# Second layer laid out anew on every engine, with turned contexts kept in DRAM

## What is computed

```python
x = x + L0_xattn(layernorm(x), ctx, key mask)          # 16 heads of 8, biases
x = x + L0_ffn(layernorm(x))                           # 8 experts, the best 2 per row
x = x + L1_xattn(layernorm(x), ctx, query mask)        # below
x = x + L1_ffn(layernorm(x))                           # relu(x @ w1 + b1) @ w2 + b2

def L1_xattn(x, context, mask):
    k, v = split(context @ Wkv); q = x @ Wq
    dots = q k^T * 64**-0.5 - (1 - mask) * 1e6         # mask on the query row
    return softmax(dots) @ v @ Wout + bout
```

## Time and profile before

| | us |
|---|---|
| median of 3 runs (lowest, highest) | 933.73 (932.86, 934.0) |
| the profiled execution | 935.8 |
| its span, from first to last instruction | 934.1 |

### The profile page before, as it was taken

The page is one execution under the profiler, slowest core; times in us unless marked ns, Lnnn a source line. Parts: engine busy times, 40 slices in busy tenths (PEclk is TensorE's granted clock), DMA queues, the critical chain, the costliest instruction groups (busy, mean ns, idle before and its releaser), DMA issues.

```text
span 934.1 us, 28124 instructions
## 1 busy us (share of the span) xinstructions
PE 838.8 (90%) x7885; PEld 748.4 (80%) x7885; DVE 672.0 (72%) x2052; ACT 673.9 (72%) x2662; POOL 453.1 (49%) x765
## 2 busy tenths in 40 slices
PE   5899999999989789999985788889899999999985
PEld 3677888787777689999984788778788888889874
DVE  5789999999988432222236877878898888988862
ACT  2999999999989423333357877787788887888860
POOL 3135545545444521111156566666666667667441
PEclk9999999999999989999997898899999999999987
DMA  5897777778777122222215666676677777777761
GB/s 165 240 247 230 227 238 238 226 237 247 229 247 179 35 88 68 67 68 73 85 34 166 212 209 199 204 222 215 198 231 225 226 219 204 238 223 234 212 208 45
DMA packets 160451, 171.93 MB, mean 184 GB/s; under 512 B 16052, under 2 KB 139318, under 8 KB 160374
## 3 DMA queue, kind: packets, MB, share of 16 engines
q1 hardware_dynamic: 153474, 156.77, 55.0%
q0 software_dynamic: 6112, 13.90, 5.7%
q10 hardware_dynamic: 788, 0.39, 0.1%
HBM read 90.87 MB, written 80.13 MB: 183 GB/s over the span
## 4 chain that ended last, share of the span: by engine, by line
PE 56%; DVE 10%; issue 9%; ACT 9%; DMA 7%; SPq 4%; POOL 3%; DVEq 0%; ACTq 0%; POOLq 0%
PE bank L1376 7%; PE bank L1383 7%; PE bank L1426 6%; PE bank L1217 6%; ACT PR L701 6%; PE bank L1171 5%; PE bank L1416 4%; PE bank L1209 4%; PE bank L1404 3%; DMA turned_blocks<-BT 3%; ACT PR L708 3%; DVE nmx L894 3%; PE bank L1328 3%; PE bank L1288 2%; PE bank L1193 2%
## 5 line engine op out<-in xcount | busy, mean ns | idle before, releaser
L701 ACT ACTIVATE PR<-PR,nmx 128x128 f32<-128x128 f32 x512 | 197.4, 401 | 0.0
L347 POOL TENSOR_TENSOR PR<-PR,rden 128x512 f32<-128x512 f32 x128 | 133.1, 1040 | 118.4 <-DVE rden L899 118.4
L701 ACT ACTIVATE PR<-bank,nmx 128x128 f32<-128x128 f32 x512 | 187.8, 431 | 0.4 <-DVE nmx L894 0.4
L701 ACT ACTIVATION_READ_ACCUMULATOR PR<-bank,nmx 128x1 f32 x512 | 139.0, 271 | 0.0
L1404 PE MATMUL bank<-XCT,wqk 128*128 128x128 f32 x832 | 115.5, 289 | 14.1 <-DVE YT L1055 10.0
L1404 PEld LDWEIGHTS bank<-XCT,wqk 128*128 128x128 f32 x832 | 103.3, 198 | 22.3 <-DVE YT L1055 11.4
L894 DVE TENSOR_REDUCE nmx<-PR 128x4 f32<-128x512 f32 x128 | 81.5, 679 | 49.8 <-ACT PR L708 49.7
L795 ACT ACTIVATE H<-bank 128x512 f32<-128x512 f32 x70 | 41.8, 597 | 90.3 <-PE bank L1376 90.3
L701 ACT ACTIVATION_READ_ACCUMULATOR PR<-PR,nmx 128x1 f32 x512 | 103.2, 202 | 0.0
L1171 PEld LDWEIGHTS bank<-ident,PR 128*128 128x128 f32 x512 | 60.9, 142 | 39.6 <-issue 37.6
L708 ACT ACTIVATE PR<-bank,fill_q 128x512 f32<-128x512 f32 x128 | 77.8, 688 | 20.4 <-PE bank L1416 20.2
(11 more groups left out here) (182 smaller groups left out, 2050.7 us busy)
## 6 DMA issues: line engine op xcount, KB each, us to landing
turned_blocks<-BT SPq DMA_DIRECT2D x64, 512.0 KB, 4.0
w<-turned_blocks SPq DMA_DIRECT2D x256, 128.0 KB, 3.1
second_layer_values<-wide SPq DMA_DIRECT2D x32, 512.0 KB
wide<-second_layer_values SPq DMA_DIRECT2D x32, 512.0 KB, 5.6
expert_outputs<-HF SPq DMA_DIRECT2D x32, 256.0 KB
expert_outputs<-HF SPq DMA_DIRECT2D x64, 128.0 KB, 2.2
KBD<-expert_outputs SPq DMA_DIRECT2D x64, 128.0 KB
QS<-expert_outputs SPq DMA_DIRECT2D x32, 256.0 KB
```

Of the source, the lines that this page charges most:

```text
L347: nc.gpsimd.tensor_tensor(unit, unit, rden[:, p, G * g:G * g + G].unsqueeze(2).broadcast_to([P, G, P]), ALU.mult).then_inc(s["nm"], 1)
L701: last = nc.scalar.activation(PR[:, g, j * P:(j + 1) * P], scored, ACT.Exp, bias=nmx[:, p, h:h + 1], accum_out=den[:, p, h:h + 1])
```

## The change

Three things are changed; what is computed stays.

- **Turned contexts.** In the first layer the SyncE queue stores each turned context `XCT[:, p, 1, :]` to a new DRAM tensor, one transfer of 64 KB for each sequence. The second layer loads from there into `XCT` directly: its `transpose_in` turns XN alone. The early contexts are loaded turned as well, and `turn_contexts` and `read_contexts` go.
- **Order in a step.** Every engine's `step1` is rewritten. Units 2 and 3 of a sequence are reduced and exponentiated in the next step; the turns of all four units stand in the next step; the XND of a sequence comes one step later, early in it; the projection of quarter 2 of sequence n + 1 stands before the scores of n.
- **Banks and readers.** Quarters 0 to 3 go to banks 5, 4, 4, 6 (before 4, 5, 6, 4), and heads to banks 6 and 5. ScalarE reads quarter 2 and VectorE reads 0, 3 and 1. The experts' rows are added one step earlier, and both halves of the turned blocks are loaded one behind the other after the second half's store.

```diff
 SyncE, step0 (first layer) and step1
+                if exists(n + 2):
+                    wait_apart(sp, (a["xct"], n + 3))
+                    sp.dma_start(ct_dram[n + 2], XCT[:, p, 1, :]).then_inc(a["cst"], 16)
...
                 if exists(n - 1):
+                    wait(sp, c["pv"], NU * (n - 2))
+                    sp.dma_start(V1[:, q, :, :].rearrange("p h d -> p (h d)"), v_dram[n - 1]).then_inc(c[f"v{q}"], 16)
+                if exists(n + 2) and not early(n + 2):
+                    wait(sp, c["y"], NU * n + NU)
+                    sp.dma_start(XCT[:, p, 1, :], ct_dram[n + 2]).then_inc(c[f"ctx{p}"], 16)
+                if exists(n - 1):
+                    store_blocks(n - 1, 1)
                     load_turned(n - 1, 0)
-                    store_blocks(n - 1, 1)
-                if exists(n + 2) and not early(n + 2):
-                    load_ctx(sp, c, n + 2, p)
-                if exists(n):
-                    wait(sp, c["pv"], NU * (n - 1))
-                    sp.dma_start(V1[:, p, :, :].rearrange("p h d -> p (h d)"), v_dram[n]).then_inc(c[f"v{p}"], 16)
-                if exists(n - 1):
                     load_turned(n - 1, 1)
 ScalarE, step1
-                if exists(n):
-                    act.wait_ge(c["y"], NU * n + NU)
...
                 if exists(n + 1):
-                    read_xct(c, n + 1, q, not early(n + 1), c["y"], NU * n)
+                    read_xct(c, n + 1, q, False, c["y"], NU * n)
+                if exists(n - 1):
+                    fill_rows(n - 1, 3)
+                    exponentials(c, n - 1, q, 2)
+                    exponentials(c, n - 1, q, 3)
+                if exists(n + 1):
+                    act.wait_ge(c["y"], NU * (n + 1) + 2)
...
+                if exists(n):
+                    fill_rows(n, 0)
+                    fill_rows(n, 1)
                 if exists(n - 2):
                     read_heads(n - 2, p, 0)
                     read_heads(n - 2, p, 1)
                 if exists(n):
-                    for g in range(NU):
-                        fill_rows(n, g)
-                    for g in range(NU):
-                        exponentials(c, n, p, g)
+                    exponentials(c, n, p, 0)
+                    fill_rows(n, 2)
+                    exponentials(c, n, p, 1)
 GpSimd, step1
-                if exists(n - 1):
-                    scale_pool(pool, c, n - 1, q, 3)
...
+                if exists(n - 2):
+                    scale_pool(pool, c, n - 2, p, 3)
+                if exists(n + 1):
...
+                    nc.gpsimd.tensor_tensor(xrow, xrow, out_bias[:, 0, :], ALU.add).then_inc(c["bias"], 1)
...
+                if exists(n - 1):
+                    scale_pool(pool, c, n - 1, q, 0)
+                if exists(n - 3):
+                    norm_pool(pool, d, n - 3, q)
...
+                if exists(n - 1):
+                    scale_pool(pool, c, n - 1, q, 1)
+                    scale_pool(pool, c, n - 1, q, 2)
 TensorE, step1
+                    wait(pe, c["x"], upto(n - 3))
+                    transpose_in(c, n + 1, q, False)
...
+                    project_y(n, p, 3)
+                    if not early(n):
+                        wait(pe, d["x"], upto(n - 4))
+                        wait(pe, c["yq"], upto(n))
+                        project_y(n, p, 1)
+                if exists(n + 1):
+                    pe.wait_ge(c["xct"], n + 2)
...
+                        project_y(n + 1, q, 0)
...
+                    project_y(n + 1, q, 2)
```

More of the change, by code:

```diff
@@ L1172, in transpose_unit @@
                 last.then_inc(s["t"], 1)
-            def turn_contexts(group, contexts, first_bank, other_bank):
-                pe.wait_ge(ld_kv if group == 0 else ld_gate, 32)
-                count = KEYS_A if group == 0 else KEYS_AHEAD - KEYS_A
-                for i in range(count):
-                    turned = nc.tensor.transpose((first_bank[:, i * P:(i + 1) * P] if i < 4 else other_bank[:, (i - 4) * P:(i - 3) * P]),
-                                                 contexts[:, i, :], ident[:])
-                turned.then_inc(set_pe, 1)
-            def project_keys(m, half):
-                first, out = (0, (bank[6], bank[1])) if m < KEYS_A else (KEYS_A, (bank[0], bank[1]))
-                if m == first:
-                    pe.wait_ge(set_copy, 3 if m < KEYS_A else 4)
-                else:
-                    pe.wait_ge(kg["kc"], 2 * m + half - 1)
+            def project_keys(m, half):
+                first, out, contexts = (0, (bank[6], bank[1]), CTX_A) if m < KEYS_A else (KEYS_A, (bank[0], bank[1]), CTX_B)
+                if m == first and half == 0:
+                    pe.wait_ge(ld_kv if m < KEYS_A else ld_gate, 32)
+                wait(pe, kg["kc"], 2 * m + half - 1)
                 for j in range(G):
@@ L1193, in project_keys @@
                     projected = mm(out[half][:, j * P:(j + 1) * P], wqk1[:, 1, chunk * P:(chunk + 1) * P],
-                                   CT[:, m - first, :], start=True, stop=True)
+                                   contexts[:, m - first, :], start=True, stop=True)
                 projected.then_inc(kg["k"], 1)
@@ L1385, in _ @@
             total = starts[NE]
-            turn_contexts(1, CTX_B, bank[3], bank[6])
             for m in range(KEYS_A, KEYS_AHEAD):
@@ L1405, in project_y @@
                                   XCT[:, p, 1 - g // 2, :], start=True, stop=True)
-                    last.then_inc(c["y"], 3 if g == 2 and early(m) else 1)
+                    last.then_inc(c["y"], 2 if early(m) else 1)
                 def scores(m, p, pair):
@@ L1425, in values @@
                             half = slice(DH1 * r, DH1 * r + DH1)
-                            last = mm(bank[5 + pair][half, j * P:(j + 1) * P].rearrange("p (i b) -> p i b", i=4),
+                            last = mm(O1_BANK[pair][half, j * P:(j + 1) * P].rearrange("p (i b) -> p i b", i=4),
                                       V1[:, p, 2 * (G * pair + j) + r, :], PTC[:, pair, :, G * r + j, :], start=True, stop=True)
@@ L1451, in step1 @@
                     pe.wait_ge(c[f"v{p}"], loads(n - 2, p))
-                    if not early(n):
-                        wait(pe, c["yc"], upto(n, 3, 0))
+                    wait(pe, c["yc"], upto(n, 3, 2))
                     if isinstance(n, int):
@@ L1457, in step1 @@
                     wait(pe, c["pt1"], 64 * (n - 1))
-                    wait(pe, c["yc"], upto(n, 3, 2))
+                    if not early(n + 1):
+                        wait(pe, c["yc"], upto(n + 1, 3, 0))
                     if isinstance(n, int):
```

219 lines of the change are left out of this document (95 added, 124 removed).

## The result

The changed kernel takes 889.91 us (884.11 to 891.61, 4 runs) where the kernel before takes 933.87 us beside it: a ratio of 0.9515, 95% interval 0.9467 to 0.9562. The forecast was 893.7 us. The sum was close, but several of its terms were not. The profiled execution took 891.61 us, its span is 890.0 us.

What follows compares the result with a forecast made beforehand. Steady steps were taken as nearly TensorE's own, early ones as a ring of waits. Terms -20.6, -7.7, -14.0 and +2.2 sum to -40.1: 934.1 to 894.0, less 0.4 for the median, 893.7 us; range 878 to 913.

Steps and rivals of the forecast that it cites:

- Early steps: Second layer, sequences 3 to 11: the wait for XND goes, steps fall from 13.58 to 11.0 us; -20.6 us.
- One sign that I had named: ScalarE in the second layer: its copies should show no waits of a microsecond.
- Turned blocks: Second-layer loads behind the second store: 8.9 us fit before the values need them, 1 to 3 us spare; cost 0.
- rival D: Turned blocks come late for the values in every step, 1.9 us of wait each; 953 us, slower; chance 0.06.
- Steady steps: Second layer, sequences 11 to 31: context transpose and bank wait go, steps fall from 13.00 to 12.3 us; -14.0 us.
- Ramp: First three steps of the second layer: three rounds of ScalarE's 10.5 us, 31.5 instead of 39.25; -7.7 us.
- SyncE's queue: First layer: the added store's issue holds up loads behind it, 0.56 us in four steps; +2.2 us.
- Between the stages: Before the second layer's first scores: 2.0 us of context transposes and copies go, hidden by sequence 1's late rows; 0 us.
- Tail: End of the second layer: later last exponentials against an earlier store of the last half; 0 us, ends -4 and +3.
- Rival B: Second layer: GpSimd holds up one more VectorE instruction by 0.7 us a step; 907 us; chance 0.15.
- Rival C: Early steps: TensorE's clock still falls once in each, so they take 11.9 us; 901 us; chance 0.09.
- Rival F: Second layer: waits only move to the next engine, both kinds of step keep their length; 934 us; chance 0.03.

Runs made afterwards that it cites:

- XND put back: Changed kernel with XND's normalisation moved from third in VectorE's step to right ahead of the copy into XDT; 966.39 us, ratio 0.9937 to the kernel before.
- the small load: Changed kernel with the second layer's load of values cut from 512 KB to 32 KB a step; 878.66 us against the changed kernel's 884.46.
- the kernel with fewer matmuls: Changed kernel without 3 of 4 matmuls of one projection group in the 20 steady steps; 890.06 us against the changed kernel's 884.46.
- the store two places ahead: Changed kernel with the first layer's store of turned contexts issued two places earlier in SyncE's step; 906.59 us, ratio 0.9357 to the kernel before.
- the second run: The changed kernel measured again, unaltered; 884.46 us where the kernel before takes 932.43, ratio 0.9481.

## Why the prediction was right, point by point

- **Early steps, -20.6 forecast, -17.0 measured (13.58 to 11.46).** The mechanism was right and is shown: XND put back takes 1.4 us a step, and the wait of the earlier trace rows is 0.2 us at most. The 11.0 us were missed by the term that I had set to nothing, the turned blocks: 7.1 / 8 = 0.9 us a step. Without them an early step would have 10.6 us; with the small load it has 10.65, of which 0.35 are still such waits. One sign that I had named failed with it: ScalarE's copies of heads waited up to 1.4 us for values whose blocks were late.
- **Turned blocks, 0 forecast.** The step of the prediction that failed: "4.0 + 1.8 + 3.1 = 8.9 us fit, with 1 to 3 us to spare". I added landings of the old, slower steps. With the same bytes in 11 us the store takes 4.5 and the loads 4.1 to land (4.0 and 3.1 in the earlier trace rows), and eight issues take 4.9 to 6.5 us together; the spare time is gone. It was rival D in small: not 1.9 us in each step but 0.9 in the early ones and almost none in the steady ones.
- **Steady steps, -14.0 forecast, -25.4 measured (13.00 to 11.73), past the term's end of -18.** "That puts TensorE at 12.88 - 0.74 = 12.14 us" was too high: its work is 11.60. I had taken the 12.88 us less the listed wait for work. A listed wait is shorter than what it costs: in the kernel with fewer matmuls 0.67 us of them (6 of the rows' matmuls, 0.112 us from start to start) went, the step lost 0.04 us, and the listed wait was 0.52. And the row of 24 matmuls from 770.70 to 773.78 us, which I read as three groups of 1.03 us of work, holds a wait. Its matmuls start 0.112 us apart, which makes 0.89 a group; once there are 0.41 us between two of them, where TensorE stood for the final addition. The gap is too short to split the row, but the waits of before, 634 to 894 us, have it:

```profile
PE bank L1404 <- DVE QF L1107: 2.2, 8, 0.3
```

In the changed kernel the four groups take 3.73 us from 730.02 to the next transpose. What I had added for the mean over an undisturbed step, 0.16 us, was right in size: 11.73 against 11.60.
- **Ramp, -7.7 forecast, -10.5 measured,** a little past its end; 28.8 us for three steps is less than three rounds of ScalarE's 10.5 us. The first two steps take 8.6 and 8.7 us; why was not tested.
- **SyncE's queue, +2.2 forecast, +2.5 (1 to 4) in the timed ratio of the slower sort.** The profile pair shows +4.4, which is no more than the scatter of equal code. The mechanism, loads held up behind the store's issue, is not shown: the store two places ahead made no difference there, and the longer waits for QS on the faster sort only agree with it.
- **Between the stages, 0 (-2 to +1) forecast, +1.0 measured and -0.4 in the second run,** from the experts' last group of matmuls to the first scores: 20.6 us before, 21.6 and 20.2 after. The first rows are normalised 1.1 us sooner behind the experts. The bias addition ahead of a gather, which I had priced at one microsecond at most, takes 0.9 of it back: it waits for XN itself, and gather, deviation and the next rows stand behind it in a chain, so the rows of sequence 1 come 4.7 us behind those of 0 (485.59 to 490.29 us) where before has 3.8 (479.75 to 483.55). The rest is the last projections, 3.43 us for 16 matmuls in this trace and 1.95 in the second run's. Most of the 8.0 us by which the first scores are later is the first layer (4.4) and the experts' stage, whose code is the same: 2.5 us longer in this trace, 0.3 in the second.

```profile
486.02 0.45 POOL L658 TENSOR_TENSOR X<-X,out_bias 128x128 f32<-128x128 f32 x1 [0.47 <-DVE XN L316]
...
490.29 0.35 DVE L316 TENSOR_SCALAR XN<-X,mv,rstd 128x128 f32<-128x128 f32 x1 [2.73 <-POOL rstd L311]
```

- **Tail, 0 forecast, +0.8,** within its ends.
- **Rival B, VectorE and GpSimd in each other's way.** It went the other way. Groups of VectorE in steady steps, 655 to 845 us:

```profile
L1070 DVE SCALAR_TENSOR_TENSOR X<-QF,gate,X 128x128 f32 x27 | 8.5, 314 | 0.0
L331 DVE TENSOR_SCALAR XND<-X,mv,rstd 128x128 f32 x13 | 4.4, 339 | 0.0
```

In the steady steps the additions take 314 ns where they took 558, and XND, 1054 ns in each early step before, takes 338 in those steps now. VectorE is busy 28 us less for the same instructions. The Trainium skill, SBUF — State Buffer, "SBUF: two separate sides", tells of an exclusive lock; that the same instruction takes 0.34 or 1.05 us by what GpSimd does beside it agrees with it, and what was a risk for me was a gain of the change. One early step of before, both engines:

```profile
614.47 1.04 POOL L347 TENSOR_TENSOR PR<-PR,rden 128x512 f32<-128x512 f32 x1
614.54 1.05 DVE L330 TENSOR_SCALAR XND<-X,mv,rstd 128x128 f32<-128x128 f32 x1
```

XND starts 0.07 us behind the unit and ends 0.08 us behind its end. It ends so in all 30 steps of before in which a unit was running when it started, whether it had then 0.97 or 0.44 us to go. In the changed kernel XND never meets a unit, and in the steady steps an addition starts 0.16 us ahead of one and takes its 0.32 us, while the unit takes 1.06 us instead of 1.04. So the order of starts decides, and here being late costs VectorE much and GpSimd nearly nothing.
- **Rival C, the clock.** 1.00 in early steps, except behind the long wait for turned blocks, where the stretch has 0.84.
- **Rival F** is refuted by the time; the kernel with fewer matmuls shows where it begins to be true: there a wait did move into the place of the work.

The total came within 4 us because terms missed in opposite directions: steady steps gave 11.4 us more and the ramp 2.8 more than forecast; early steps gave 3.6 less, and the time up to the first scores cost 5.8 more (8.0 instead of 2.2, of which some is the scatter of stages that the order doesn't touch). That part of the agreement is luck.

## What to carry to other kernels

When steps become shorter, the same bytes have to pass in less time: take the landing times of a spacing argument at the new rate, not from the old trace. When an engine's work is read off a trace as step minus listed waits, the short gaps and hand-overs stay in it, and a merged row can hold a wait too short to be listed; sum up the start-to-start times of single instructions instead. When every other step is longer in a loop that holds two steps, compare it with the steps written out behind the loop before looking for a ring. And in a ring that several engines close, one short instruction on which a transpose waits (0.34 us of VectorE), put in the wrong place, can take back most of what a reordering gains, while an engine that is full need not be the only bound.

## What was not expected of the hardware

- Two sorts of chip: the kernel before takes 932 to 934 us on one and 969 to 975 on the other, at equal durations of single instructions. The changed order takes 884 to 890 on the first; its variants take 907 to 912 on the second. The slower sort loses some 18 us in the first layer and, in each looped step of the second, 1.0 us in the old order and 0.25 in the new one; in the experts' stage and in the new order's steps behind the loop it loses nothing.
- The end of one and the same first layer lies between 311.7 and 316.2 us from one profiled execution to the next (five of them), 0.5% of the whole: a difference of 4 us between two traces, in a stage of 310 us, is no finding.
- With the DMA engines 91% busy in the early steps (256 GB/s), a store of 512 KB took 4.4 us to land; with 0.48 MB less in each step (84% and 223 GB/s), 3.0.
- XND, 0.34 us alone, took 0.52 to 1.05 us where it started behind a unit of GpSimd, and ended 0.08 us behind it each time.
- VectorE stood idle for 0.25 us where its loop of two steps turns back.
